# A planned attention kernel: order of the opening, four norms on ScalarE, new places

## The chip, the cores and the metric

One core of one Trainium2 chip. The metric is the device time of one execution in microseconds (us), lower is better.

## The reference

`x` is (4, 2048, 256) in FP32: 4 batches, 2048 tokens, width 256. Three residual steps:

```python
x = x + 0.5 * ffn(layernorm(x))      # 8 experts, top 2; an expert with more than cap tokens gives 0
x = x + attn(layernorm(x))           # 16 heads of 16, window of 128 each way, token 0 global
x = x + 0.5 * ffn(layernorm(x))
```

`cap` is int(1.25 * 8192 / 8) = 1280 tokens. An expert that gets more is left out as a whole (`keep = counts <= cap`). In attention, query and key may meet if they are at most 128 apart or one of them is token 0; logits are scaled by 1/4, softmax, times V, times Wo. `layernorm` has no gain or bias, eps 1e-5.

## The kernel before, in words

The kernel computes attention straight through and, beside it, the gate's logits for both expert steps; at the end a flag says whether any expert is kept. Only then are the experts computed and attention done over. In the profiled execution this part does not run: what is timed is attention, the logits, and the flag.

A batch is 16 tiles of 128 tokens in 4 chunks of 4 tiles; heads go in 4 groups of 4, so there are 16 groups (4 batches times 4), each over 16 tiles. The work of one chunk:

- EARLY: load x; MOMENTS per tile on VectorE (bn_stats, bn_aggr, L716, L718); RSTD on GpSimd (L730 to L743: rstd by pow, the shift); NORM per tile, (x - mean) * rstd into `xn`. In batch 0 all NORMs are on VectorE (L1387), in later batches tiles 0 and 1 on GpSimd (L1280), 2 and 3 on ScalarE (L1167).
- XT: two transposes of two tiles each on TensorE (L900) into one of two shared PSUM banks, emptied by ScalarE (XT_IN, L1191) into `xnT`.
- QK: q and k of a group of heads for one chunk, 4 parts of 8 matmuls (L965), into a shared bank. FP32 operands are then cut into three BF16 pieces: PIECE1 on ScalarE (L1209), REST on VectorE (L1463, which frees the bank), PIECE2 on ScalarE (L1224), PIECE3 on GpSimd (L1327).
- STACK: 12 DMAs stack the pieces along the contraction axis, as `q_stack` and `k_stack`. They are issued by SP. In group 0 five of the twelve are issued by ScalarE (L1218), in its own order between its other work.
- A: the logits of a strip of 128 queries of one head, 4 matmuls (L1076), in a ring of three PSUM banks; VectorE adds the mask and takes the row maximum (L1535, two records per strip). 1024 strips in all. The maxima are turned (TURN_MAX), split (MAX, PIECES) and laid into `q_stack` by 3 more DMAs (L870).
- B, 20 tiles behind A: the logits again, transposed and less the maximum (L1110), exp on ScalarE (L1259), masks CUT on GpSimd (L1339, L1344). PV, three tiles later (L1128), then TURN, OUT_ADD, OUT_RECIP, OUT_MULT.
- VALUES (L980) makes V; FIRST, in nine stages, is the row of token 0, which meets all keys.
- LATE: per chunk, once its batch's attention is done: TURN_ATTN (L933), PROJECT (L947), the residual on VectorE (PROJECT_IN, L1443), MOMENTS, RSTD, the second logits, STORE.

The order is written by `stages` and `schedule`. Time is counted in quarters: one quarter is one strip of A, 64 make a group, 256 a batch. The tables (`QK_AT`, `VALUES_AT`, `FIRST_AT`, `EARLY`, `LATE`, `LOAD_AT` and so on) give a quarter for each step; in batch 0 tables ending in `_OPENING` are used, and negative quarters lie ahead of the first strip. `schedule` sorts all steps into one list, and each engine runs through that list and takes its own steps in that order. An engine never goes past a step whose semaphore is not there. So the tables set only the order on each engine, and waiting sets the times. The two shared banks (`misc`) are handed out in list order too: a step gets the bank that was emptied longest ago, and waits (`claim`) until it is.

Ahead of the first real matmul TensorE runs `keep_busy(WARM)`: matmuls of ones by ones (L885, two records each) into a bank that nobody reads. `BUSY_XT[c][p]`, `BUSY_QK[c]` and `BUSY_A` put more of them before the transposes, the QKs of group 0 and the first strips; they are issued ahead of the waits of the step they stand before.

```python
def norm_engine(i, t):

    return "vector" if first and order[i][1] == 0 else NORM_ENGINES[t // 2]
```

ScalarE's order in the opening is: XT_IN of chunk 1 (twice), PIECE1, PIECE2, STACK 0 0, XT_IN of chunk 2 (twice), PIECE1, PIECE2 of it, XT_IN of chunk 3 (twice), STACK 0 1, PIECE1 of chunk 3, and so on. Chunks are counted from 1 in this text and from 0 in the code's tuples: A 2 2 is head 2 of tile 2.

## Time and profile before

| what | us |
|---|---|
| three timed runs | 842.47, 846.52, 848.89 |
| their median | 846.52 |
| the profiled execution, its own time | 843.41 |
| its span in the profile | 841.6 |

The span is from the first to the last instruction that the profiler recorded; the execution's own time has 1.8 us more around it. "Busy" is the union of an engine's instruction records; a busy TensorE is not TensorE at its peak, since the ends of matmuls are modelled. The chain of waits is followed back from the last instruction, at each step to what released it. The granted clock is 1.00 for 2.4 GHz and 0.50 for 1.2 GHz.

### The profile page before, as it was taken

How to read it: one execution, taken by the hardware profiler on the slowest of the kernel's cores; microseconds unless marked ns; L12 is line 12 of the kernel's file. 1: busy time of each engine (PE TensorE's matmuls, PEld its weight loads, DVE VectorE, ACT ScalarE, POOL GpSimd, SP SyncE). 2: the span in 40 equal slices, each digit the busy share in tenths (PEclk: the TensorE clock that was granted, in tenths of full speed). 3: DMA queues.
4: the chain of work that ended last, by engine and by line, in shares of the span. 5: the costliest groups of instructions: out<-in, count | busy, mean ns of one | idle time of the engine just before them, and what ended most of it. 6: DMA issues, size and time to landing. Idle time of an engine off the chain costs nothing.

```text
span 841.6 us, 50562 instructions
## 1 busy us (share of the span) xinstructions
PE 809.3 (96%) x21494; PEld 618.2 (73%) x21495; DVE 730.9 (87%) x2787; ACT 610.3 (73%) x1387; POOL 524.5 (62%) x888
## 2 busy tenths in 40 slices
PE   7899999999999999999999999999999999999997
PEld 7655767778788787677778777777778778776675
DVE  6899899998977899998987799998987789999864
ACT  3325778897877667888777766888787766788970
POOL 2355756896554556888554466789554465766772
PEclk9999999999999999999999999999999999999999
DMA  8342225332213235442222244533221323424003
GB/s 240 90 98 68 83 76 135 112 112 69 82 59 117 91 116 151 123 130 69 89 94 66 82 143 129 148 98 100 68 79 62 114 95 103 134 78 128 7 28 107
DMA packets 93210, 83.55 MB, mean 99 GB/s; under 512 B 17584, under 2 KB 92208, under 8 KB 92976
## 3 DMA queue, kind: packets, MB, share of 16 engines
q1 hardware_dynamic: 91376, 78.91, 30.7%
q8 instruction: 172, 2.82, 1.5%
q10 hardware_dynamic: 1600, 1.31, 0.8%
q14 instruction: 62, 0.51, 0.2%
HBM read 20.66 MB, written 8.39 MB: 35 GB/s over the span
## 4 chain that ended last, share of the span: by engine, by line
PE 76%; DVE 9%; ACT 6%; issue 3%; POOL 3%; SPq 1%; ACTq 1%; DMA 1%; DVEq 0%; POOLq 0%
PE bank L1128 15%; PE bank L1076 12%; PE bank L1110 12%; PE bank L965 11%; PE bank L947 7%; PE bank L980 6%; DVE bank L1535 5%; PE bank L1150 3%; ACT probs L1259 3%; PE bank L933 2%; PE bank L885 2%; PE bank L900 1%; ACT pieces L1209 1%; PE bank L1020 1%; DVE row_max L1535 1%
## 5 line engine op out<-in xcount | busy, mean ns | idle before, releaser
L1259 ACT ACTIVATE probs<-bank 128x384 f32<-128x384 f32 (+1 forms) x1024 | 457.1, 479 | 144.1 <-PE bank L1110 127.6
L1535 DVE CUSTOM_DVE_ANT_0 bank<-bank,con 128x288 f32<-128x288 f32 x1024 | 493.4, 514 | 58.4 <-PE bank L1076 52.4
L1076 PE MATMUL bank<-k_stack,q_stack 96*32 96x288 bf16 x4096 | 334.1, 288 | 7.1 <-DVE row_max L1535 4.2
L1110 PE MATMUL bank<-q_stack,k_stack 99*32 99x288 bf16 (+3 forms) x4096 | 326.3, 284 | 5.8 <-ACT probs L1259 2.1
L1128 PE MATMUL bank<-probs,v_sb 128*32 128x128 f32 x5888 | 314.5, 272 | 4.6 <-issue 1.7
L1339 POOL TENSOR_SCALAR_AFFINE_SELECT probs<-probs 128x512 f32<-128x512 f32 x240 | 154.7, 644 | 135.4 <-ACT probs L1259 134.4
L1128 PEld LDWEIGHTS bank<-probs,v_sb 128*32 128x32 f32 x5888 | 200.8, 110 | 34.3 <-issue 5.8
L1076 PEld LDWEIGHTS bank<-k_stack,q_stack 96*32 96x32 bf16 x4096 | 134.8, 95 | 68.1 <-DVE row_max L1535 25.2
L1110 PEld LDWEIGHTS bank<-q_stack,k_stack 99*32 99x32 bf16 x4096 | 131.1, 95 | 57.1 <-ACT probs L1259 34.4
L1344 POOL TENSOR_SCALAR_AFFINE_SELECT probs<-probs 128x512 f32<-128x512 f32 x240 | 152.8, 637 | 21.1 <-ACT probs L1259 21.1
L965 PE MATMUL bank<-xnT,wqk_sb 128*32 128x256 f32 x2048 | 160.3, 379 | 0.1
L1535 DVE DVE_READ_ACCUMULATOR2_ANT row_max<- 128x1 f32 x1024 | 143.6, 140 | 0.0
L1327 POOL TENSOR_TENSOR pieces<-rest,pieces 128x512 bf16<-128x512 f32 x64 | 74.6, 1166 | 62.1 <-ACT pieces L1224 62.1
L980 PE MATMUL bank<-wv_sb,xnT 128*32 128x272 f32 x1024 | 86.1, 393 | 0.6 <-DVE rest L1463 0.2
L947 PE MATMUL bank<-wo_sb,attnT 128*32 128x264 f32 x1024 | 73.9, 386 | 0.7 <-DVE x_ring L1443 0.4
L965 PEld LDWEIGHTS bank<-xnT,wqk_sb 128*32 128x32 f32 x2048 | 65.8, 110 | 5.2 <-ACT v_sb L1231 0.5
L1209 ACT ACTIVATE pieces<-bank 128x512 bf16<-128x512 f32 x64 | 38.4, 600 | 25.6 <-PE bank L965 24.4
L1463 DVE TENSOR_TENSOR rest<-bank,pieces 128x512 f32<-128x512 f32 x64 | 44.0, 688 | 8.2 <-ACT pieces L1209 8.0
L1224 ACT ACTIVATE pieces<-rest 128x512 bf16<-128x512 f32 x64 | 40.6, 634 | 8.6 <-DVE rest L1463 8.4
L1150 PE MATMUL bank<-con,o_raw 128*32 128x68 f32 x2048 | 44.5, 223 | 1.6 <-ACT o_raw L1266 1.6
L1266 ACT ACTIVATE o_raw<-bank 128x512 f32<-128x512 f32 x59 | 35.2, 596 | 11.8 <-PE bank L1128 11.7
L1356 POOL TENSOR_TENSOR glob_term<-v_all,p 128x272 f32<-128x272 f32 x64 | 41.6, 650 | 3.2 <-DVE v_all L1504 2.8
(124 smaller groups left out, 738.3 us busy)
## 6 DMA issues: line engine op xcount, KB each, us to landing
q_stack<-pieces SPq DMA_DIRECT2D x384, 64.0 KB
k_stack<-pieces SPq DMA_DIRECT2D x364, 64.0 KB
x_ring<-in_x SPq DMA_DIRECT2D x28, 512.0 KB, 5.3
out_x<-x_ring SPq DMA_DIRECT2D x15, 512.0 KB, 3.7
attn<-in_x SPq DMA_DIRECT2D x4, 512.0 KB, 6.2
wback_sb<-in_wback SPq DMA_DIRECT2D x8, 256.0 KB, 5.5
k_stack<-pieces ACTq DMA_DIRECT2D x20, 64.0 KB
q_stack<-neg_max SPq DMA_DIRECT2D x48, 16.0 KB, 2.4
```

Source lines behind the costliest of these rows:

```text
L947: last = pe.matmul(bank_of("PROJECT", i, t)[SP * s:SP * (s + 1), 0:D + E], attnT[:, t // 2, k, at:at + SP], wo_sb[:, k, :], start=(k == 0) ...
L965: last = pe.matmul(bank_of("QK", g, c)[SP * s:SP * (s + 1), 256 * half:256 * (half + 1)], wqk_sb[:, g % NG, k, SP * s:SP * (s + 1)], xnT[: ...
L980: last = pe.matmul(bank_of("VALUES", b, t)[SP * s:SP * (s + 1), 0:D + HD], xnT[:, k, at:at + SP], wv_sb[:, k, :], start=(k == 0), stop=(k ...
L1076: last = pe.matmul(a_ring[i % len(a_ring)][SP * s:SP * (s + 1), 0:WIN], q_stack[g % 2][0:KROWS, h, q:q + SP], k_stack[g % 2][0:KROWS, h, q ...
L1110: last = pe.matmul(score_bank(i)[SP * s:SP * (s + 1), start:final], k_stack[g % 2][0:SROWS, h, WINDOW + P * j + SP * s:WINDOW + P * j + SP ...
L1128: last = pe.matmul(o_bank[SP * h:SP * (h + 1), P * (i % 4):P * (i % 4 + 1)], v_sb[:, j, VW * head:VW * head + SP], probs[:, j % 4, h, P * ...
L1150: last = pe.matmul(bank_of("TURN", n)[SP * s:SP * (s + 1), HG * VW * i:HG * VW * (i + 1)], o_raw[:, at:at + SP], take, start=True, stop=True)
L1259: act.activation(probs[:, j % 4, h, c0:c1], score_bank(i)[:, c0:c1], ACT.Exp, scale=LOGIT_SCALE).then_inc(S["exp_ready"], 1)
L1327: pool.tensor_tensor(pieces[i % PIECES][:, 2, :], rest[:, :], pieces[i % PIECES][:, 1, :], ALU.subtract).then_inc(S["piece3_ready"], 1)
L1339: pool.affine_select(out=part, in_=part, compare_op=ALU.is_ge, fill=0.0, base=0, pattern=[[0, HG], [1, P]], channel_multiplier=-1).then_in ...
L1344: pool.affine_select(out=part, in_=part, compare_op=ALU.is_ge, fill=0.0, base=0, pattern=[[0, HG], [-1, P]], channel_multiplier=1).then_in ...
L1535: dve.tensor_tensor_reduce(out=a_ring[i % len(a_ring)][:, 0:WIN], in0=a_ring[i % len(a_ring)][:, 0:WIN], in1=mask, scale=1.0, scalar=con[: ...
```

## The change

It changes the tables that set the order, nearly all of them, and three rules. WARM goes from 31 to 27, the fillers before the second transpose of chunk 1 from 4 to 1, those before its QK from 3 to 1. `NORM_FIRST` puts tiles 2 and 3 of chunks 3 and 4 of batch 0 on ScalarE instead of VectorE (4 instructions). Batch 0 gets its own table `EARLY_FIRST` for MOMENTS, RSTD and NORM. The second copy of a transpose in batch 0 stands one quarter later. No other instruction is added, dropped or changed.

Worked out from the tables, the order of the opening on VectorE was, from the moments of chunk 2 on: REST of chunk 1, MOMENTS 2 0, NORM 1 0, NORM 1 1, MOMENTS 2 1, NORM 1 2, MOMENTS 2 2, MOMENTS 2 3, NORM 1 3, then MOMENTS of chunk 4 mixed with NORM of chunk 3, REST of chunk 2, NORM 2 3, NORM 3 0 to 3 3, seven strips, REST of chunk 3, strips to A 4 2, REST of chunk 4. It is now: MOMENTS 2 0, REST of chunk 1, MOMENTS 2 1, NORM 1 0, NORM 1 1, MOMENTS 2 2, MOMENTS 2 3, NORM 1 2, NORM 1 3, NORM 2 0, NORM 2 1, MOMENTS 3 0 to 3 3, REST of chunk 2, NORM 3 0, NORM 3 1, nine strips, REST of chunk 3, strips to A 4 3, REST of chunk 4. (First number: chunk from 0; second: tile.)

On ScalarE NORM 2 2 and 2 3 stand behind the copies of chunk 2 and ahead of its PIECE1; NORM 3 2 and 3 3 stand behind the copies of chunk 3 and ahead of the DMA issues of STACK 0 1 and of PIECE1 of chunk 3. PIECE2 of chunk 3 stands behind the first copy of chunk 4. On TensorE the QK parts of chunks 3 and 4 stand one to two strips later. On SP some loads and stores pass one stack or one MAX.

```diff
--- before.py
+++ after.py
@@ -349,9 +349,9 @@
         LEAD = 3
         STACK_DMAS = 2 * TERMS
         MAX_STACKED = 16 * 3
-        WARM = 31
-        BUSY_XT = ((0, 4), (0, 5), (0, 8), (0, 3))
-        BUSY_QK = (3, 4, 0, 0)
+        WARM = 27
+        BUSY_XT = ((0, 1), (0, 5), (0, 8), (0, 3))
+        BUSY_QK = (1, 4, 0, 0)
         BUSY_A = ((0, 0, 0, 1),)
 
 
@@ -372,35 +372,37 @@
 
             return (P if j == 0 else 0), (2 * P if j == NT - 1 else 3 * P)
 
-        QK_AT = (-43, -28, -10, 5, 23, 41, 53, 68, 83, 101, 118, 134, 149, 165, 178, 202)
+        QK_AT = (-43, -25, -10, 5, 23, 40, 53, 68, 83, 99, 118, 134, 149, 165, 179, 202)
         QK_APART = (2, 3, 2, 2, 2, 2, 1, 3, 1, 1, 1, 1, 1, 1, 2, 2)
         ONES_FROM = 2
         STACK_LAG = 20
-        VALUES_AT = (33, 48, 57, 61, 69, 80, 88, 94)
-        VALUES_APART = (2, 2, 1, 2, 2, 2, 1, 2)
-        VALUES_AT_OPENING = (36, 47, 57, 63, 66, 80, 89, 94)
-        VALUES_APART_OPENING = (1, 1, 1, 0, 2, 1, 1, 0)
+        VALUES_AT = (33, 47, 57, 61, 71, 80, 88, 94)
+        VALUES_APART = (2, 1, 0, 2, 2, 2, 1, 2)
+        VALUES_AT_OPENING = (36, 47, 57, 63, 67, 76, 89, 93)
+        VALUES_APART_OPENING = (1, 1, 1, 0, 2, 2, 0, 1)
         LOGITS_LAG = -2
-        FIRST_AT = (-16, -8, 15, 32, 50, 60, 96, 111, 135)
-        FIRST_AT_OPENING = (10, 22, 32, 44, 50, 60, 103, 106, 137)
-        FIRST_APART = (1, 2, 1, 4, 1, 3, 0, 1, 4)
-        EARLY_AT = (-79, -64, -49, -31)
-        EARLY = {'LOAD': -18, 'MOMENTS': (0, 3, 6, 7), 'RSTD': 10, 'NORM': (11, 13, 14, 18), 'XT': 19}
+        FIRST_AT = (-16, -9, 15, 32, 53, 60, 96, 111, 139)
+        FIRST_AT_OPENING = (10, 19, 32, 44, 50, 60, 103, 106, 138)
+        FIRST_APART = (1, 3, 1, 1, 0, 4, 0, 1, 0)
+        EARLY_AT = (-79, -64, -48, -31)
+        EARLY = {'LOAD': -20, 'MOMENTS': (-1, 3, 6, 7), 'RSTD': 9, 'NORM': (10, 13, 13, 18), 'XT': 19}
         NORM_ENGINES = ("gpsimd", "scalar")
-        EARLY_AT_OPENING = (-68, -49, -39, -30)
-        XT_AT_OPENING = (-55, -31, -18, 9)
-        QK_AT_OPENING = (-44, -26, 2, 14, 25, 39, 52, 69, 85, 98, 124, 131, 153, 162, 182, 201)
-        OPENING = {'ORDER_HEADS': -79, 'WBACK': -53, 'FOLD': 175, 'FILL': 21, 'QK_APART': 1, 'STACK': 5, 'STACKS': 12}
+        EARLY_FIRST = {'MOMENTS': (1, 3, 7, 7), 'RSTD': 7, 'NORM': (12, 13, 15, 15)}
+        NORM_FIRST = (('vector', 'vector'), ('vector', 'vector'), ('vector', 'scalar'), ('vector', 'scalar'))
+        EARLY_AT_OPENING = (-62, -47, -41, -29)
+        XT_AT_OPENING = (-50, -32, -16, 9)
+        QK_AT_OPENING = (-44, -25, 4, 15, 25, 39, 52, 70, 84, 98, 124, 131, 153, 165, 182, 201)
+        OPENING = {'ORDER_HEADS': -78, 'WBACK': -62, 'FOLD': 175, 'FILL': 13, 'QK_APART': 1, 'STACK': 7, 'STACKS': 11}
         LATE_AT = (95, 115, 131, 146)
         LATE_AT_END = (52, 68, 85, 102)
-        LATE = {'LOAD': -13, 'TURN_ATTN': 2, 'PROJECT': ((7, 8, 10, 10), (12, 12, 15, 15)), 'BASE': -13, 'MOMENTS': (12, 18, 18, 19), 'RSTD': 21, 'STORE': 25}
+        LATE = {'LOAD': -17, 'TURN_ATTN': 2, 'PROJECT': ((7, 8, 10, 11), (12, 12, 15, 15)), 'BASE': -15, 'MOMENTS': (12, 16, 19, 19), 'RSTD': 25, 'STORE': 27}
         LATE_END = {'TURN_ATTN': 0, 'PROJECT': ((6, 6, 8, 9), (12, 15, 15, 15)), 'BASE': -2, 'MOMENTS': (12, 16, 16, 23), 'RSTD': 35, 'STORE': 24}
-        LOAD_AT = (150, 164, 188, 214, 351, 346, 373, 388, 417, 427, 445, 459, 572, 610, 627, 635, 646, 678, 685, 717, 863, 869, 891, 907, 988, 1000, 1006, 1129)
-        STORE_AT = (381, 396, 400, 416, 618, 641, 659, 679, 878, 923, 916, 937)
-        WBACK_AT = (214, 471, 723)
+        LOAD_AT = (152, 155, 186, 215, 354, 350, 374, 380, 411, 414, 435, 450, 573, 608, 630, 632, 642, 673, 685, 718, 867, 876, 896, 906, 999, 995, 986, 1119)
+        STORE_AT = (371, 390, 396, 422, 628, 642, 654, 679, 882, 930, 919, 936)
+        WBACK_AT = (212, 469, 723)
         COUNT_AT = 16
         FLAG_AT = (6, 6)
-        OUT_AT = (-1, -1, 4, 3, -1, -1, -1, 1, -1, 8, 1, 0, 0, 1, 3, 0)
+        OUT_AT = (-1, -1, 4, 3, 0, -1, -1, 1, -1, 8, 1, 0, -1, 1, 3, 0)
         OUT = {'TURN': 0, 'ADD': 0, 'RECIP': 1, 'MULT': 2}
         MAX_AT = {'KEY0': -1, 'TURN_MAX': 1, 'MAX': 2, 'PIECES': 3, 'P0': -1, 'EXP0': 6}
 
@@ -429,13 +431,13 @@
                     early = BATCH * b + EARLY_AT[c] if b else EARLY_AT_OPENING[c]
                     late = BATCH * (b + 1) + (LATE_AT if b < nb - 1 else LATE_AT_END)[c]
                     moments = (LATE if b < nb - 1 else LATE_END)["MOMENTS"][0]
-                    order.append((early + EARLY["MOMENTS"][0], "EARLY", b, c, early))
+                    order.append((early + (EARLY if b else EARLY_FIRST)["MOMENTS"][0], "EARLY", b, c, early))
                     order.append((late + moments, "LATE", b, c, late))
             order = [item[1:] for item in sorted(order, key=lambda item: item[0])]
             ringed = [i for i, (phase, b, _, _) in enumerate(order) if phase == "LATE" or b]
 
             for i, (phase, b, c, at) in enumerate(order):
-                plan = EARLY if phase == "EARLY" else LATE if b < nb - 1 else LATE_END
+                plan = (EARLY if b else EARLY_FIRST) if phase == "EARLY" else LATE if b < nb - 1 else LATE_END
                 if first and i in ringed:
                     begun = LOAD_AT[ringed.index(i)]
                     end(begun, "LOAD", i)
@@ -462,11 +464,11 @@
                     end(at + plan["RSTD"], "RSTD", i)
                 if phase == "EARLY":
                     for t in range(4):
-                        opening(at + EARLY["NORM"][t], "NORM", i, t)
+                        opening(at + plan["NORM"][t], "NORM", i, t)
                     turn = at + EARLY["XT"] if b else XT_AT_OPENING[c]
                     for p in range(2):
                         begin(turn, "XT", i, p)
-                        opening(turn + 1, "XT_IN", i, p)
+                        opening(turn + 1 + (0 if b else p), "XT_IN", i, p)
             for n in range(NG * nb):
                 b, g = divmod(n, NG)
                 for c in range(4):
@@ -681,7 +683,7 @@
 
             def norm_engine(i, t):
 
-                return "vector" if first and order[i][1] == 0 else NORM_ENGINES[t // 2]
+                return NORM_FIRST[order[i][2]][t // 2] if first and order[i][1] == 0 else NORM_ENGINES[t // 2]
 
             def gates(i):
```

## Rows read from the trace of the kernel before

**Rows 1.** The page: busy time by engine, VectorE's strips (busy, mean ns, idle)
```profile
PE 809.3 (96%) x21494; PEld 618.2 (73%) x21495; DVE 730.9 (87%) x2787; ACT 610.3 (73%) x1387; POOL 524.5 (62%) x888
...
L1535 DVE CUSTOM_DVE_ANT_0 bank<-bank,con 128x288 f32<-128x288 f32 x1024 | 493.4, 514 | 58.4 <-PE bank L1076 52.4
```

**Rows 2.** Stretches: us, busy PE, PEld, DVE, ACT, POOL (records), clock, DMA share, GB/s
```profile
0.00:40.00 40.00, 33.84 (x430) 27.20 (x431) 28.10 (x103) 12.19 (x19) 13.35 (x29) 0.96 0.61 169
40.00:80.00 40.00, 37.74 (x787) 21.97 (x791) 39.14 (x158) 15.04 (x35) 18.86 (x21) 1.00 0.32 83
80.00:720.00 640.00, 627.97 (x17215) 488.28 (x17209) 568.25 (x2212) 499.93 (x1138) 419.07 (x713) 1.00 0.33 100
```

**Rows 3.** Chain that ended last, 0 to 41 us: start, length, what
```profile
1.15 9.55 PE bank L885 x62
...
13.13 1.91 PE bank L965 x32
...
18.42 0.35 DVE stats L716
...
20.29 0.39 DVE xn L1387
...
23.43 1.86 PE bank L965 x32
...
27.67 0.45 PE bank L900 x4
...
32.51 0.60 ACT pieces L1209
...
39.38 0.61 ACT pieces L1209
```

**Rows 4.** PE's fillers (us, PE, PEld busy, clock, DMA), and a transpose
```profile
7.00:10.60 3.60, 3.60 (x34) 3.50 (x32) 1.00 1.06 353
20.00:23.00 3.00, 1.93 (x10) 1.85 (x10) 0.50 0.90 101
...
18.48 0.66 PE L900 MATMUL bank<-con,xn 128*128 128x128 f32 x4 [3.48 <-DVE xn L1387]
```

**Rows 5.** VectorE in order of time, opening
```profile
8.53 1.38 DVE L1387 TENSOR_SCALAR xn<-attn,mean_var,rstd 128x256 f32<-128x256 f32 x4 [1.48 <-POOL rstd L733]
...
15.69 0.69 DVE L1463 TENSOR_TENSOR rest<-bank,pieces 128x512 f32<-128x512 f32 x1 [3.64 <-ACT pieces L1209]
...
29.50 0.52 DVE L1535 CUSTOM_DVE_ANT_0 bank<-bank,con 128x288 f32<-128x288 f32 x1
...
29.94 0.52 DVE L1535 CUSTOM_DVE_ANT_0 bank<-bank,con 128x288 f32<-128x288 f32 x1
...
33.13 0.69 DVE L1463 TENSOR_TENSOR rest<-bank,pieces 128x512 f32<-128x512 f32 x1 [0.82 <-ACT pieces L1209]
...
40.01 0.69 DVE L1463 TENSOR_TENSOR rest<-bank,pieces 128x512 f32<-128x512 f32 x1 [0.55 <-ACT pieces L1209]
```

**Rows 6.** Groups by line: normalising on VectorE (opening) and on ScalarE (later batches)
```profile
L1387 DVE TENSOR_SCALAR xn<-attn,mean_var,rstd 128x256 f32<-128x256 f32 x16 | 6.8, 468 | 2.7 <-POOL rstd L733 2.2 <-PE bank L900 0.6
...
L1167 ACT ACTIVATE xn<-x_ring,shift,rstd 128x256 f32<-128x256 f32 x24 | 14.3, 594 | 0.0
```

**Rows 7.** ScalarE and its DMA issues (ACTq), 26 to 41 us
```profile
28.15 0.60 ACT L1191 ACTIVATE xnT<-bank 128x512 f32<-128x512 f32 x1 [0.31 <-PE bank L900]
28.15 4.30 ACTq L1218 DMA_DIRECT2D k_stack<-pieces  x5
...
34.64 0.55 ACTq L1218 DMA_DIRECT2D k_stack<-pieces  x1
...
35.23 4.05 ACTq L1218 DMA_DIRECT2D k_stack<-pieces  x4
```

**Rows 8.** Waits of GpSimd and PE, 120 to 760 us: total, times, longest
```profile
POOL var_eps L730 <- DVE mean_var L718: 3.9, 9, 0.7
...
PE bank L1128 <- POOL probs L1339: 0.7, 1, 0.7
```

## The prediction

> **What bounds the kernel now.** I read the page first. TensorE (PE) is busy 96% of the 841.6 us span and VectorE (DVE) 87% [rows 1]. The middle of the kernel (80 to 720 us) has 640.0 - 628.0 = 12.0 us in which PE is idle; the first 40 us alone have 6.2 us, with every other engine far from full, and from 40 to 80 us DVE is busy 39.1 of 40 us [rows 2]. So three things set the end: a serial chain in the opening, DVE just behind it, and PE's plain work after that, which no order shortens. A time saved before DVE fills at about 40 us should move everything behind it, since what follows is issued in a fixed order against semaphores.
>
> So the chain of the opening is what I read closest [rows 3]. In it the reader is to see: 62 filler records of PE (31 matmuls) up to 10.70, then transposes with fillers between them, QK of the first chunk from 13.13, the pieces on ScalarE (ACT) and DVE, a DVE stretch of moments and normalisations up to 20.68, transposes and fillers up to 23.43, QK of chunk 2, fillers again, a last transpose up to 28.12, and from 28.15 on ACT: a copy, five DMA issues, PIECE1 at 32.51, REST on DVE at 33.13, then the same once more, to PIECE1 at 39.38 and REST at 40.01.
>
> **The opening, step by step.** (a) WARM drops by 4 matmuls, 8 records. The fillers at 7.0 to 10.6 run 34 in 3.60 us, 0.106 each [rows 4], so the first transpose comes 0.85 earlier, at 9.85. Its data is there: DVE normalises from 8.53, two tiles by about 9.3, four by 9.91 [rows 5]. The fillers before the second transpose go from 4 to 1, 6 records or 0.64 less, and it starts at about 10.5, behind the 9.91 at which its tiles are ready. QK needs the ACT copy of that transpose, 0.60 [rows 7], so it starts at about 11.6 where it started at 13.13. The fillers before QK (3 to 1) lie beside that copy and are worth nothing. Sum: 1.5 us earlier. It cannot be more, because the 9.91 and the copy are next in line.
>
> (b) MOMENTS of tile 0 of chunk 3 now stands ahead of REST. DVE is idle there (3.64 us before REST [rows 5]) and the chunk's load has most of the time since 5.8 to land, so it costs nothing and takes 0.55 from behind REST. But MOMENTS of tile 1 takes its place there, so the first transpose of chunk 2 gains nothing beyond 1.5. Behind it stood MOMENTS, NORM, MOMENTS, MOMENTS, NORM (18.42 to 20.68, 2.26 [rows 3]); now MOMENTS, MOMENTS, NORM, NORM, some 1.9, since the first MOMENTS is gone ahead and the rest stand side by side. The tiles of the second transpose are thus ready 1.9 earlier.
>
> (c) The stretch 20.0 to 23.0 ran at a granted clock of 0.50, that is 1.2 GHz: 10 fillers in 1.93 us, 0.193 against 0.106 [rows 4]. It came after PE had been idle from 15.04 to 18.48 [rows 3, 4]. The gap keeps its size, so I let the slow stretch come again at the same step, and carry 1.9 us to the end of the second transpose of chunk 3, 28.12 to 26.2. If the slow stretch missed the transpose and the fillers, both would take half (1.1 and 1.6 us there): 0.55 + 0.8 more, 3.3 in all. If it fell on QK instead, the gain would be 1.5. I keep 1.9, with 1.5 and 3.3 as ends.
>
> (d) Two tiles each of chunks 3 and 4 are normalised on ACT. DVE's 0.47 becomes ACT's 0.59 [rows 6]; ACT's row is of later batches, with x_ring as the source and the same 128x256 shape. For chunk 3 the two (1.2 us) lie in ACT's idle time before PIECE1 and cost nothing. For chunk 4 they stand between the copy of the last transpose and the five DMA issues. Those begin with the ACT instruction ahead of them (both at 28.15, [rows 7]) and take 4.30, and PIECE1 is queued behind them. The issues start at 26.25 + 0.5 + 0.55 = 27.3, end at 31.6, and PIECE1 comes at 31.65 instead of 32.51. So of 1.9 us some 1.1 is given back, and 0.86 is left. Ends: nothing given back (the norms lie under the issue time) and 1.2 given back.
>
> (e) REST of chunk 3 now stands two strips later in DVE's order. DVE idled 0.82 before it with 7 strips done; the strips cost 0.44 each (29.50 to 29.94) [rows 5]. Now 9 are done when REST runs. Against that PE's second transpose of chunk 4 still waits for the bank that REST frees, at about 32.9, so the tenth and eleventh strip can't run on freely: strip A 2 2 runs at about 33.75 instead of 35.05 (33.13 + 0.6 + 3 times 0.44), 1.3 earlier. For REST of chunk 4, ACT's copy (33.55) starts the next five issues, 4.64 from first to last [rows 7], so PIECE1 comes at 38.25 instead of 39.38, and DVE has one strip more done: 1.1 + 0.44 = 1.55 us earlier at 40 us. From there DVE is full and all shifts together. PIECE2 behind the first copy costs nothing, as REST is not done before the copy is.
>
> **The rest.** Behind the opening QK, VALUES, FIRST, PROJECT and MOMENTS move by a few places in each batch, some loads and stores pass one stack, and RSTD of the early chunks is one place earlier, a place being one strip, at most 0.8 us (841.6 over the 1024 strips of [rows 1]). No instruction is added or taken away. Where PE is full, an exchange on it is worth nothing; where it isn't, only the 12.0 us of [rows 2] can be won. The loads and stores that pass a stack wait for other data than it does; what SP loses or wins there the trace does not show, and the bounds cover it. I put all this at 0, with ends -4.0 (a third of the 12.0 won) and +3.2 (the second rival).
>
> Sum against the profiled execution: 843.41 - 1.55 = 841.9. That execution is 3.1 below the median 846.52, inside the spread 842.47 to 848.89; off the median the sum gives 845.0. I take the middle, 843.4.
>
> The Trainium skill has a rule that speaks about step (d): "DMA: Bandwidth & Descriptors", section "Issuing engines are not separate DMA queues", says that issuing on several engines only saves sequencer time, usually small beside the transfer. By it the ACT issues would hardly matter and 1.1 us would not be given back (840.8 from 843.41, 842.3 by the middle); the row with 4.30 us of issues ahead of PIECE1 says otherwise, and I go by the row.
>
> **Rivals.**
> 1. The clock takes the gain. With fewer fillers PE has less to do before each QK. For it: the clock did fall to 0.50 after the one long gap [rows 4]. Against: only 9 matmuls go, and the new gap before QK of chunk 1 is some 0.4 us. If the slow stretch covered QK of chunk 2 (1.86) as well as what it covers now, the QK would take up to 1.86 more, of which 1.55 eats the gain: time unchanged, 843.41 by the profile, 845.0 where the forecast has 843.4. The Trainium skill, "TensorE: Matmul & The Clock Gate", section "Part 1: The HAM clock gate (the "warmup" mystery)", has it that slow is the default and that activity releases it; by that rule taking fillers out is the wrong way. This rival has its chance from it and the row together.
> 2. The other side: GpSimd (POOL) blocked. RSTD of the early chunks of batches 2 to 4 waits for moments of DVE, whose last place is unchanged while RSTD's is one earlier. In 120 to 760 us it already waited 3.9 us in 9 of its 24 turns [rows 8]. Up to 0.8 more in each of 12 is 9.6 us of waiting on POOL, with the masks (CUT) of the probabilities queued behind it, and PE's PV behind them. PE's own wait for POOL there is 0.7 us [rows 8], so most of it is hidden. If a third comes through, 3.2: 843.41 - 1.55 + 3.2 = 845.1, 1.7 slower than before (846.6 where the forecast has 843.4). It decides from 1.55 us, a sixth of the added waiting, on.
> 3. The middle gains. If each of three batches recovers 1.0 to 1.3 us of its PE idle time (12.0 in 640 us) through the new places, the time is 3.0 to 4.0 lower: 838 to 839 by the profile, 840 to 841 where the forecast has 843.4. For it: nearly all tables of the batches are re-made. Against: PE is at 98% there.
> 4. The change doesn't do what it says: the norms on ACT give back all the opening saves. The ends of (c) and (d), 1.5 - 1.2, leave 0.3, and the strip ahead 0.4: 0.7 less, 842.7 by the profile, 844.3 where the forecast has 843.4, not told apart from my forecast by the time, only by the trace.
>
> **How the numbers follow.** Forecast with rival 4 0.50, rival 1 0.14, rival 2 0.14, rival 3 0.20, something larger of either sign 0.02. The range is 838.0 to 848.5: below, rival 3 with half of the runs' own spread; above, rival 2 with 2.2 of it. What a measurement can tell from no change is about 1%, 8.5 us; none of these cases reaches it alone, rival 3 on a low sample comes nearest. Hence faster 0.09, same 0.86, slower 0.05.
>
> **What would show it.** In the changed profile: the filler group 54 records; QK of chunk 1 at 11.6; the second transpose of chunk 2 by 19.9; 4 NORM records on ACT before 30 us, the latter two ending just before or beside the issues; PIECE1 of chunk 3 at 31.7, REST of chunk 4 at 38.9, PE idle in the first 40 us about 4.5 to 5. If REST of chunk 4 is not earlier than 39.5, the opening is wrong; if it is and the span isn't shorter by as much, it is the middle, and the waits of POOL for moments tell whether rival 2 is it.

## The result, and the profile after

The changed kernel takes **846.1 us** (median of 22 runs, 843.12 to 853.85), the kernel before 843.0 us (22 runs, 840.38 to 849.51). The ratio is **1.0033, 95% interval 1.0018 to 1.0049**: some 2.8 us slower by the means. I had forecast 1.6 us faster. The time lies inside my range; the sign is wrong.

The page's head and first block, after, as [rows 1]:

```profile
span 844.6 us, 50526 instructions
...
PE 810.7 (96%) x21476; PEld 613.5 (73%) x21477; DVE 731.4 (87%) x2783; ACT 614.0 (73%) x1391; POOL 524.8 (62%) x888
```

And the stretches, as [rows 2] (us, busy PE, PEld, DVE, ACT, POOL, clock, DMA share, GB/s):

```profile
0.00:40.00 40.00, 33.50 (x460) 26.79 (x462) 29.41 (x109) 14.99 (x24) 14.69 (x31) 0.91 0.65 174
40.00:80.00 40.00, 38.87 (x807) 22.34 (x808) 38.87 (x157) 17.58 (x41) 19.42 (x22) 1.00 0.32 86
80.00:720.00 640.00, 626.70 (x17141) 481.92 (x17133) 567.58 (x2203) 498.23 (x1130) 415.65 (x706) 1.00 0.33 99
720.00:830.00 110.00, 103.11 (x2946) 77.31 (x2948) 89.92 (x302) 82.60 (x198) 75.04 (x131) 0.98 0.22 71
```

Busy time says little here. PE is busy 626.7 of the middle's 640 us where it was 628.0; four NORMs have gone from DVE to ACT and nothing else shows. What shows is the place of the work in time. The chain of waits in the opening, as [rows 3]:

```profile
9.39 0.63 PE bank L902 x4
10.02 0.22 PE bank L887 x2
10.24 0.44 PE bank L902 x4
10.90 1.91 PE bank L967 x32
...
16.25 1.12 PE bank L902 x4
17.36 2.13 PE bank L887 x10
19.50 0.85 PE bank L902 x4
20.35 1.71 PE bank L887 x8
22.06 1.86 PE bank L967 x32
...
26.30 0.44 PE bank L902 x4
```

QK of chunk 1 starts at 10.90 where it started at 13.13. REST on DVE, as [rows 5]:

```profile
13.46 0.69 DVE L1465 TENSOR_TENSOR rest<-bank,pieces 128x512 f32<-128x512 f32 x1 [0.81 <-ACT pieces L1211]
...
31.33 0.69 DVE L1465 TENSOR_TENSOR rest<-bank,pieces 128x512 f32<-128x512 f32 x1
...
37.79 0.69 DVE L1465 TENSOR_TENSOR rest<-bank,pieces 128x512 f32<-128x512 f32 x1
```

REST of chunk 4 comes at 37.79 instead of 40.01, with one strip more done. So at 40 us the changed kernel is 2.7 us ahead, more than forecast, and at the end it is 3.0 us behind. To see where that went I took the start of the same strip on DVE (L1535 before, L1537 after, 1024 records each in the timeline) in each profile and subtracted that of before:

| strip | 0 | 64 | 256 | 448 | 512 | 640 | 768 | 896 | 1003 | 1023 | end |
|---|---|---|---|---|---|---|---|---|---|---|---|
| changed kernel | -1.9 | -3.0 | -3.0 | -0.8 | -1.9 | -2.6 | -0.9 | +0.1 | 0.0 | +2.3 | +3.0 |

The opening's 3 us hold through batch 1 and are lost in batches 2 to 4 and in the tail. The tail's part is one stop of TensorE, here in its timeline (start, length, what, idle before and what ended it):

```profile
773.97 0.30 PE L1112 MATMUL bank<-q_stack,k_stack 99*32 99x288 bf16 x4
774.09 0.29 PE L1078 MATMUL bank<-k_stack,q_stack 96*32 96x288 bf16 x3
776.30 0.40 PE L1078 MATMUL bank<-k_stack,q_stack 96*32 96x288 bf16 x1 [1.91 <-issue]
776.30 0.82 PE L1130 MATMUL bank<-probs,v_sb 128*32 128x128 f32 x8
```

PE stands still for 1.91 us after three of the four matmuls of one strip. The fourth needs no tile that the third did not, and the profile shows no semaphore that it waited for ("issue"). Then the clock falls, in PE's windows:

```profile
776.30:779.70 3.40, 3.40 (x61) 0.51 0.03 8
779.70:782.00 2.30, 2.30 (x76) 0.99 0.00 0
```

3.4 us at 0.51 (1.2 GHz) do the work of 1.7 us at full clock. Stop and slow stretch together are 3.6 us, a little more than the span's whole loss.

### The profile page after: what moved, and what is told of

It reads as the page before. It is cut to its first block, busy times and chain, and to the rows that moved or that the text cites. A ratio compares the mean times of both kernels' runs of the same rounds, so it can differ in the third digit from the quotient of the medians.

```text
span 844.6 us, 50526 instructions
## 1 busy us (share of the span) xinstructions
PE 810.7 (96%) x21476; PEld 613.5 (73%) x21477; DVE 731.4 (87%) x2783; ACT 614.0 (73%) x1391; POOL 524.8 (62%) x888
## 4 chain that ended last, share of the span: by engine, by line
PE 71%; DVE 14%; ACT 5%; issue 4%; POOL 3%; SPq 1%; DMA 1%; ACTq 0%; POOLq 0%; DVEq 0%
PE bank L1130 15%; PE bank L1112 12%; PE bank L1078 12%; PE bank L967 11%; DVE bank L1537 8%; PE bank L949 6%; PE bank L982 6%; PE bank L1152 3%; ACT probs L1261 3%; PE bank L935 2%; DVE row_max L1537 2%; PE bank L902 1%; DVE rest L1465 1%; DVE stats L718 1%; ACT pieces L1211 1%
## 5 line engine op out<-in xcount | busy, mean ns | idle before, releaser
L1537 DVE CUSTOM_DVE_ANT_0 bank<-bank,con 128x288 f32<-128x288 f32 x1024 | 495.0, 516 | 65.2 <-PE bank L1078 58.7
L1537 DVE DVE_READ_ACCUMULATOR2_ANT row_max<- 128x1 f32 x1024 | 144.8, 141 | 0.0
L982 PE MATMUL bank<-wv_sb,xnT 128*32 128x272 f32 x1024 | 83.2, 393 | 0.5 <-DVE rest L1465 0.2
L949 PE MATMUL bank<-wo_sb,attnT 128*32 128x264 f32 x1024 | 76.0, 387 | 0.7 <-DVE x_ring L1445 0.4
L1152 PEld LDWEIGHTS bank<-con,o_raw 128*32 128x32 f32 x2048 | 36.0, 108 | 10.1 <-ACT o_raw L1268 7.6
```

Of the source, the lines that this page charges most:

```text
L949: last = pe.matmul(bank_of("PROJECT", i, t)[SP * s:SP * (s + 1), 0:D + E], attnT[:, t // 2, k, at:at + SP], wo_sb[:, k, :], start=(k == 0) ...
L982: last = pe.matmul(bank_of("VALUES", b, t)[SP * s:SP * (s + 1), 0:D + HD], xnT[:, k, at:at + SP], wv_sb[:, k, :], start=(k == 0), stop=(k ...
L1152: last = pe.matmul(bank_of("TURN", n)[SP * s:SP * (s + 1), HG * VW * i:HG * VW * (i + 1)], o_raw[:, at:at + SP], take, start=True, stop=True)
L1537: dve.tensor_tensor_reduce(out=a_ring[i % len(a_ring)][:, 0:WIN], in0=a_ring[i % len(a_ring)][:, 0:WIN], in1=mask, scale=1.0, scalar=con[: ...
```

## The experiments

18 kernels ran, in five comparisons, each with its own runs of the kernel before (medians 844.18, 843.58, 842.86, 844.31 and 842.59). "Mean" is the mean of the kernel's runs less that of before in the same comparison. Single executions of one kernel scatter by about 2 us (standard deviation), so a mean of this table has a standard error of 0.5 to 0.9 us, and two kernels in different comparisons are told apart from some 2 us on.

| kernel | median us | ratio, 95% interval | mean |
|---|---|---|---|
| open_only | 841.9 | 0.9965 [0.9943, 0.9986] | -2.5 |
| batch_only | 850.4 | 1.0064 [1.0040, 1.0087] | +5.6 |
| after_loads_late | 848.72 | 1.0051 [1.0026, 1.0076] | +4.5 |
| before_loads_late | 846.63 | 1.0029 [1.0004, 1.0055] | +2.3 |
| open_sp_new | 845.77 | 1.0015 [0.9991, 1.0038] | +1.2 |
| open_pe_new | 845.76 | 1.0019 [0.9999, 1.0040] | +2.0 |
| open_el_new | 842.29 | 0.9986 [0.9968, 1.0004] | -1.7 |
| after_sp_back | 844.4 | 1.0007 [0.9988, 1.0026] | +0.4 |
| open_qk_new | 843.29 | 0.9988 [0.9966, 1.0010] | -0.6 |
| open_values_new | 844.11 | 1.0002 [0.9971, 1.0032] | +0.8 |
| open_values_first_new | 844.3 | 1.0014 [0.9985, 1.0042] | +0.8 |
| open_out_new | 844.18 | 1.0001 [0.9974, 1.0027] | +0.2 |
| open_again | 842.19 | 0.9985 [0.9961, 1.0009] | -1.7 |
| open_warm_back | 843.03 | 0.9991 [0.9968, 1.0015] | -0.9 |
| open_norm_dve | 842.55 | 0.9982 [0.9961, 1.0002] | -1.3 |
| open_loads_spread | 843.28 | 0.9977 [0.9957, 0.9997] | -1.3 |
| after_qk_back | 845.74 | 1.0036 [1.0014, 1.0058] | +3.0 |
| after_sp_qk_back | 843.25 | 1.0024 [1.0005, 1.0042] | +1.1 |

**Opening or batches.** `open_only` is the changed kernel with the twelve tables of batches 2 to 4 (QK_AT, VALUES_AT, VALUES_APART, FIRST_AT, FIRST_APART, OUT_AT, EARLY_AT, EARLY, LATE, LOAD_AT, STORE_AT, WBACK_AT) of before; `batch_only` is the kernel before with those twelve of the changed kernel.

> The changed opening with the batch tables of before. The two profiles compared strip by strip say: the opening saves about 2.0 us up to the first strip, 2.7 up to the REST of chunk 4 and some 3.0 by the end of batch 1. Theory A (the batch tables lose it, about 1.1 us in batch 2 and some more later, and the tail has a stall of its own): this kernel is 2 to 3 us faster than before. Theory B (what loses is a stall of 1.9 us of TensorE at 774.4 us, in the middle of a strip's four matmuls, while three loads of 512 KB are in flight: TensorE has run out of instructions and its next block of them stands behind the loads; where the blocks end depends on how many filler matmuls the opening has): the stall, with up to 3.4 us at half clock behind it, is here too, and the time is within 1 us of before or above it.

> The opening of before (31 fillers, all normalisations on VectorE) with the changed batch tables. Theory A (batch tables): slower than before by 4 to 6 us, most of it between strips 336 and 450 of each batch. Theory B (instruction block behind the loads, set by the opening's instruction count): the blocks end where they did before, no stall above 1 us in 770 to 780 us, and the time is 0 to 1.5 us above before.

Measured: the opening alone wins 2.5 us, and 1.7 when built and timed anew; the batches' tables alone lose 5.6. (`batch_only`'s -0.6 at strip 64 grows to +3.7 at strip 448 and +9.9 at strip 1003.) So the loss is in the batches' tables, as theory A had it (4 to 6 us), and the opening's gain comes through where they are left alone.

**The last loads.** A first idea was that the three loads before the tail's stop cause it and that they could simply stand later:

```diff
-LOAD_AT = (..., 999, 995, 986, 1119)
+LOAD_AT = (..., 1034, 1033, 1032, 1119)
```

and in `before_loads_late` 988, 1000, 1006 became 1032, 1033, 1034.

> The changed kernel, with the loads of the last batch's chunks 1 to 3 (3 times 512 KB) issued after the 3 DMAs of MAX 15 (about 789 us) instead of right after STACK 15 3 (769 us). Nothing needs them before 808 us. Theory B: the stall of 1.9 us at 774.4 us and the half clock behind it go, the kernel is 2.5 to 4 us faster than the changed one, so about 0.5 us faster than before. Theory A: within 1 us of the changed one, 2 to 3 us slower than before.

> The kernel before with the same three loads moved behind MAX 15. There the chain shows 3.4 us for the last stack DMA and TensorE waiting 1.1 us for it at 771.2 us, with the same loads in flight. Theory B: the loads' burst costs this kernel only that: 0.5 to 1.5 us faster than before. Rival: the burst costs nothing but moves, same as before within 0.5 us.

Both got slower, which neither theory had. The stop did not go, it moved with the loads and grew. PE in the timeline of `after_loads_late`:

```profile
795.61 0.65 PE L1130 MATMUL bank<-probs,v_sb 128*32 128x128 f32 x8 [3.08 <-issue]
```

and in that of `before_loads_late` (the kernel before has no such stop in its tail; its wait of 1.09 at 771 us is one for keys and queries, and stays here with 1.18):

```profile
793.18 0.30 PE L1110 MATMUL bank<-q_stack,k_stack 99*32 99x288 bf16 x2 [2.94 <-issue]
```

That points at the loads. The page of the changed kernel has a DMA queue of kind "instruction" (packets, MB, share), and 172 of its packets of 16 KB fit PE's 21476 + 21477 records at 256 instructions each (167.8):

```profile
q8 instruction: 172, 2.82, 1.6%
```

Between 45 us and the end six in ten start 3.5 to 4.9 us apart, the mean is 4.7, and one in ten is over 6.0. The DMA view of the changed kernel, cut to 767.0 to 773.7, shows the three loads and no such packet:

```profile
GB/s 6 0 220 141 12 6 12 6 12 6 0 141 239 12 0 226 159 6 24 55 0 0 31 147 208 220 373 373 379 373 391 373 391 379 385 385 391 391 385 385
...
q1 hardware_dynamic: 1259, 1.21, 53.8%
issues: line engine op xcount, KB each, median us to landing
x_ring<-in_x SPq DMA_DIRECT2D x3, 512.0 KB, 4.9
```

The same view from 773.7 to 775.0 has it, among 368 GB/s of other traffic:

```profile
q8 instruction: 1, 0.02, 5.3%
```

I listed the stops of PE of over 0.7 us behind 45 us in all profiles, with the last instruction packet ahead of their end. The longest of eight kernels:

| kernel | stop at | us | since the packet before | packet's start to the stop's end |
|---|---|---|---|---|
| changed kernel | 774.4 | 1.91 | 7.3 | 2.5 |
| open_only | 771.4 | 1.12 | 7.1 | 2.2 |
| open_sp_new | 509.5 | 1.68 | 7.1 | 2.6 |
| open_pe_new | 134.1 | 1.44 | 7.2 | 2.6 |
| open_el_new | 563.3 | 1.08 | 8.2 | 2.6 |
| batch_only | 494.6 | 2.80 | 9.3 | 2.7 |
| before_loads_late | 790.2 | 2.94 | 8.0 | 2.4 |
| after_loads_late | 792.5 | 3.08 | 8.5 | 2.4 |

All of over 1.1 us that are put down to "issue" end 2.2 to 3.1 us after a packet, and that packet came 5.1 to 9.3 us behind the one before it. That alone proves little, as a packet in five comes over 5.5 us behind the one before it and few of them stop PE. The records can be counted, though, and that settles it. Take the number of PE's records (matmuls, weight loads and the sequencer's own) before a stop, less 256 for each instruction packet that started ahead of the last one before the stop's end. In the twenty profiles there are 160 stops of over 0.15 us put down to "issue" between 45 and 800 us, and this number is 449, 450 or 451 for every one of them: they all stand at the edge of a block of 256 instructions, in whatever strip that edge falls. PE's 750 idle times put down to a semaphore lie anywhere from 189 to 583 by the same count, 22 of them at 449 to 451. 157 of the 160 end 2.2 to 3.5 us after a packet's start. So these stops, the small ones too, are PE out of instructions; that is shown.

The same count, taken where a packet starts, tells how late it is by PE's own progress: the median is 252 records, which leaves PE some 200 (my estimate from 43,543 records in 844.6 us: 3.8 us of work). At the packet ahead of the changed kernel's stop of 1.91 us it is 430, the highest of its profile; at the packets of the stops of 2.80, 2.94 and 3.08 us it is 449, so PE was dry before they started. All 16 stops of over 1.1 us follow a packet at 365 or more. With under 50 GB/s of other traffic in the 3 us ahead of a packet the mean is 244, with over 330 GB/s it is 335. Moving the loads moved the stop, and packets start later under traffic; both are shown. That a packet waits in the DMA engines behind a load is the likely way, but no view shows its waiting. Ahead of 15 of the 16 a transfer of 512 KB was in flight; at the other (`batch_only`, 338.0, 1.21 us) two loads and a store had been issued from 327.4 us on and keys and queries followed. Ahead of its stop at 494.6 `batch_only` has SP issue two loads back to back, where the kernel before has keys and queries between them:

```profile
485.42 3.82 SPq L838 DMA_DIRECT2D x_ring<-in_x  x2
```

**Which tables.** On top of `open_only` the changed tables were put in by kind: those of SP's transfers (`open_sp_new`: LOAD_AT, STORE_AT, WBACK_AT), of TensorE (`open_pe_new`: QK_AT, VALUES_AT, VALUES_APART, FIRST_AT, FIRST_APART, OUT_AT), of statistics, norms and projections (`open_el_new`: EARLY, EARLY_AT, LATE). `after_sp_back` is the changed kernel with SP's three of before.

> The changed opening with the batches' places of before, except the places of SyncE's transfers (LOAD_AT, STORE_AT, WBACK_AT), which are the changed kernel's. With the places of before throughout, this kernel took 0.9965 of before. Theory S (the changed order of SyncE's 512 KB transfers starves TensorE of instructions): it gives back most of the 6.8 thousandths between that and the changed kernel, so about 1.000 to 1.003, with stops of TensorE of over 1 us in the middle of a strip. Theories E (VectorE's and GpSimd's places of statistics and norms) and P (TensorE's places): 0.995 to 0.998, no such stop.

> The changed opening, the batches' places of before except TensorE's (QK_AT, VALUES_AT, VALUES_APART, FIRST_AT, FIRST_APART, OUT_AT), which are the changed kernel's. Theory P: about 1.000 to 1.003 of before. Theories S and E: 0.995 to 0.998.

> The changed opening, the batches' places of before except those of the statistics, norms and projections (EARLY, EARLY_AT, LATE), which are the changed kernel's. Theory E: about 1.000 to 1.003 of before, with the turning of a group's maxima waiting some 1 us for VectorE's row of maxima behind a statistic in several groups, or GpSimd's cut behind a RSTD. Theories S and P: 0.995 to 0.998 and no such waits beyond those of before.

> The changed kernel with LOAD_AT, STORE_AT and WBACK_AT of before. Theory S: it falls to about 0.997 of before (the changed kernel took 1.0033), and the stop of 1.91 us at 774 us and the half clock after it are gone. Theories E and P: 1.001 to 1.004.

Against `open_only` and `open_again` the transfers cost 3 to 4 us, TensorE's places 4, each to about 1 us, the statistics and norms nothing. `after_sp_back` gives 2.4 back, less than theory S had said: 1.0007, not 0.997. Its stop at 774 us is down to 0.76. So S and P are both right in part, E is out.

PE's idle time at the edges of instruction blocks (45 to 800 us, stops over 0.15 us, one profile each) is 2.7 us in the kernel before, 2.8 and 2.9 in `open_only` and `open_again`, 5.6 in `open_sp_new`, 5.7 in `open_pe_new`, 4.9 in the changed kernel and 9.7 in `batch_only`. So TensorE's places seem to work in part through late instructions too. It does not come out everywhere: `after_sp_back` has 5.8, and the kernels with only one kind of TensorE's places 2.0 to 4.1. Over the twenty kernels this idle time goes with the mean time (correlation 0.7), and PE's waits for other engines and DMAs do not (-0.2).

TensorE's places were then split, again on top of `open_only`:

> The changed opening, the batches' places of before except QK_AT, which is the changed kernel's. The kernel with all of TensorE's new places lost about 4.5 us to the one with none in its strips of batches two to four, always at the same strips (about +0.6 at strips 240 to 300 and -0.8 at 304, +1 at 432, -0.8 at 480, +1.2 at 544, +1 at 752, +0.6 at 800). If the queries' and keys' places cause it, this kernel shows those steps and takes about 1.001 of before; if not, none of them and 0.996 to 0.998.

> The changed opening, the batches' places of before except VALUES_AT and VALUES_APART, which are the changed kernel's. If the values' places cause the loss of TensorE's new places: about 1.001 of before and steps at the same strips of each batch; if not, 0.996 to 0.998.

> The changed opening, the batches' places of before except VALUES_AT, VALUES_APART, FIRST_AT and FIRST_APART, which are the changed kernel's. Against the kernel with the values' places alone it tells what the first products' places do: if they cause the loss of TensorE's new places, about 1.001 of before where the values' places alone give 0.997; if neither, both 0.996 to 0.998.

> The changed opening, the batches' places of before except OUT_AT, which is the changed kernel's: the turn of the result of groups 4 and 12 stands one quarter away. If that causes the loss of TensorE's new places, about 1.001 of before; I expect none of it, 0.996 to 0.998.

The four times alone decide little (0.9988 to 1.0014, each +-0.003). The strips do show a mechanism for QK_AT. At the end of two groups DVE takes the row of maxima with the global key (KEY0). In `open_qk_new`, DVE's timeline:

```profile
345.73 1.16 DVE L1524 TENSOR_TENSOR row_max<-row_max,s0T 128x64 f32<-128x64 f32 x1
346.78 0.51 DVE L1537 CUSTOM_DVE_ANT_0 bank<-bank,con 128x288 f32<-128x288 f32 x1
```

and GpSimd's beside it:

```profile
345.62 1.16 POOL L1329 TENSOR_TENSOR pieces<-rest,pieces 128x512 bf16<-128x512 f32 x1
346.76 1.22 POOL L1282 TENSOR_SCALAR xn<-x_ring,mean_var,rstd 128x256 f32<-128x256 f32 x1
```

An instruction of 64 elements a partition takes 1.16 us and ends with GpSimd's subtraction. In the changed kernel it is 0.84, and PE, next in line, waits for it:

```profile
347.85 0.30 PE L1088 MATMUL bank<-con,row_max 128*32 128x128 f32 x2 [1.04 <-DVE row_max L1524]
```

The line's own view gives the least, median and longest of its 16 records in ns; the longest is 547 in the kernel before, 842 in the changed one, 1219 in `open_qk_new`, and in `after_qk_back` 273:

```profile
L1524 DVE TENSOR_TENSOR row_max<-row_max,s0T x16: 246/264/273, 60.9 to 780.4; 128x64 f32<-128x64 f32 x16
```

So the wait is real and QK_AT makes it. But is it the loss? The last two kernels put QK_AT back in the changed kernel, alone and with SP's three tables:

> The changed kernel (1.0033 of before) with QK_AT of before. If the queries' and keys' places put VectorE's row of maxima (0.84 us at 347 and 546 us, where GpSimd's subtraction of 1.16 us runs beside it) and TensorE's wait of 1.04 us behind it, the row takes 0.55 us at most, the wait is under 0.3 us, and the time is 1 to 2 us less: 1.001 to 1.002. If the wait has another cause it stays.

> The changed kernel with LOAD_AT, STORE_AT, WBACK_AT and QK_AT of before. If the two named mechanisms are most of the loss: 0.998 to 0.999, as the changed opening with the batches' places of before (0.9965 and 0.9985 in two measurements) and no stop of TensorE over 1 us but the one near 773 us. If the loss is spread over all of TensorE's places: 1.000 to 1.001, as with the transfers alone put back (1.0007).

The wait of 1.04 us is gone, the time is not less: 1.0036. With the transfers put back too it is 1.0024, not 0.998. The strips say why: in `open_qk_new` strips 544 to 559 take 1.0 us more than before and strips 560 to 575 take 0.7 less. The wait is mostly caught up at once.

To use all comparisons together I fitted the means of the fourteen kernels that differ by whole tables (least squares, weighted by their errors) by a sum of six parts:

| part | us | standard error |
|---|---|---|
| opening | -1.5 | 0.3 |
| SP's transfers | +2.5 | 0.5 |
| QK_AT | +0.3 | 0.4 |
| values and first products | +1.9 | 0.5 |
| turns of the result (OUT_AT) | +1.1 | 0.6 |
| statistics, norms, projections | -0.7 | 0.4 |

`open_values_new`, which has only half of the fourth part, counts for the whole of it. No kernel is more than 1.0 us off this sum; for the changed kernel it gives +3.5, measured +2.8.

**The opening's parts.** `open_again` is `open_only` unchanged; `open_warm_back` has WARM, BUSY_XT and BUSY_QK of before; `open_norm_dve` has all of NORM_FIRST on "vector"; `open_loads_spread` spreads the last burst:

```diff
-LOAD_AT = (..., 988, 1000, 1006, 1129)
+LOAD_AT = (..., 964, 980, 1006, 1129)
```

> The same kernel as open_only (the changed opening, the batches' places of before), built and timed anew. If the opening's gain carries to the end, 0.994 to 0.999 of before again; if the first measurement was luck, 1.000 to 1.002. Its profile shows how much the same program varies between two executions: less than 1 us strip for strip, apart from the opening's slow clock, if the steps that I read from single profiles are real.

> open_only with WARM, BUSY_XT and BUSY_QK of before (31 waiting products ahead of the first transposition in place of 27, more between the parts). The prediction put their removal at 1.5 us at the first queries and keys. If it holds, the first queries and keys start 1.5 us later than in open_only (10.9 us) and the strips 0.5 to 1.5 us later to the end, 0.998 of before; if the opening waits for the loads or for VectorE rather than for these products, no difference in the strips.

> open_only with the last two tiles of chunks three and four normalised on VectorE as before, at their new places. The prediction held that the tiles on ScalarE give back 1.1 us in the opening (PIECE1 of chunk three behind them) and give VectorE one more strip per norm moved. If that holds, the first strip comes 0.5 to 1.0 us earlier here; if, as the profile of the changed kernel suggests, ScalarE has room beside its five transfers, the strips come 0 to 1 us later than in open_only: four norms of 0.47 us on VectorE, about 1 us of them on the path.

> open_only with the last three loads apart (LOAD 28 ahead of the third and LOAD 29 ahead of the fourth set of key and query transfers of the last group, LOAD 30 behind them as before), in place of three back to back. Theory S' (an instruction block of TensorE that falls into a burst of 512 KB loads comes late, and TensorE stops in the middle of a strip): the stop of 0.8 to 1.9 us near 771 us, which every kernel with the changed opening shows at the same strip, goes, no two blocks near it lie over 6 us apart, and the time is 1 us less, about 0.995 to 0.997 of before. Rival (the stop is a wait of the strip for something else): it stays. Third: the loads hold up the last keys and queries and the last strips come later than in open_only.

`open_again` shows what one profile is worth: its strips differ from those of `open_only` by 0.3 at strip 64 and by 2.3 at strip 544. A step of under about 1 us in a single pair of profiles proves nothing; steps that return at the same strip in all kernels with a table do.

`open_warm_back`'s chain has QK of chunk 1 just where before has it:

```profile
12.02 0.44 PE bank L902 x4
12.45 0.67 PE bank L887 x6
13.12 1.91 PE bank L967 x32
```

and `open_again`'s, with the new filler counts:

```profile
1.14 8.39 PE bank L887 x54
9.53 0.52 PE bank L902 x4
10.05 0.22 PE bank L887 x2
10.27 0.44 PE bank L902 x4
10.71 0.22 PE bank L887 x2
10.93 1.91 PE bank L967 x32
```

The fillers are 2.2 us there, and 0.8 us in the means (-0.9 against -1.7 in the same comparison, not told apart by the time alone). Taking the norms back to DVE changes the time by nothing measurable; QK of chunk 3 starts 0.7 us later (27.8, 27.1 in `open_again`).

`open_loads_spread` does away with the stop at 771 us, and PE now stops where the first of the loads has gone:

```profile
757.01 0.31 PE L1130 MATMUL bank<-probs,v_sb 128*32 128x128 f32 x3 [1.23 <-issue]
```

The packet ahead of it came 6.9 us behind the last, where I had expected none over 6. Its mean is that of `open_norm_dve` in the same comparison, -1.3: nothing won. The stop went where a load met an instruction packet again.

## Why the prediction was wrong

**The step that failed is "The rest. ... I put all this at 0".** I argued that no instruction is added and that where PE is full an exchange on it is worth nothing. The whole of it is +5.6 us measured alone and +4.3 behind the opening (2.8 + 1.5 of the fit), above even my end of +3.2. Two things were missing from my argument. First, I looked at the transfers only for SP's own waiting ("what SP loses or wins there the trace does not show, and the bounds cover it") and not at whom a 512 KB load stands in front of. With the new places of the transfers PE's instructions come late: +2.5 us by the fit. Second, an exchange on a full engine can cost although it can't gain: a stop of PE is lost for good unless slack follows it, and 12.0 us of idle in 640 us leaves little. Of that part (+3.3 in the fit) KEY0 beside GpSimd's subtraction was seen, and the test says that it is not where the time goes; `open_pe_new` has 2.8 us more idle at block edges than `open_only`, in one profile. Which of the places of values, first products and turns does it, and how, is **open**.

**The opening's total was right, by luck: its terms were not.** Forecast -1.55, by the fit -1.5 +-0.3, by `open_only` and `open_again` -2.5 and -1.7. That 846.1 lies in my range is luck too. The range spans 10.5 us, and I took 845.0 for the kernel before, from three runs and a profile, where 22 runs give 843.0.

- (a) Fillers: forecast 1.5, measured 2.2. I said that the fillers before QK lie beside ACT's copy and are worth nothing. In both chains QK starts when those fillers end, 0.67 us behind the transpose before and 0.22 now: PE did not wait for that copy (10.05 to 11.31 for both copies, QK from 10.90). In the code the first half of QK waits only for the first copy. So these fillers were worth 0.45; most of the rest is the warm group, whose eight records moved its end by some 1.2 (10.70 before, 9.53 in `open_again`) and not by 0.85.
- (b) The second transpose of chunk 2 was forecast by 19.9 and comes at 19.50; right, although the first one starts at 16.25, 2.2 earlier and not 1.5.
- (c) The slow stretch came again, but not at the same step. It begins at about 15.2 and lasts twice as long as the 3.4 us of before:

```profile
15.20:22.00 6.80, 5.75 (x28) 0.50 0.63 122
```

The first transpose of chunk 2 takes 1.12 instead of 0.66 and its fillers 2.13. The end of the second transpose of chunk 3 is at 26.74, forecast 26.2. In the profiles of `open_again`, `open_loads_spread` and `open_norm_dve` QK of chunk 2 is at 20.8 to 21.1 instead of 22.06, with a clock of 0.83 instead of 0.76 over 10 to 20 us. So rival 1, the clock takes the gain, was right in kind: it took about 1 us in some executions, and the extra 0.7 of (a) outweighed it.
- (d) ACT's norms: 1.1 us "given back" was wrong, the true size is 0. ACT's timeline after, as [rows 7]:

```profile
26.77 0.60 ACT L1193 ACTIVATE xnT<-bank 128x512 f32<-128x512 f32 x1 [0.31 <-PE bank L902]
26.89 0.55 ACTq L1220 DMA_DIRECT2D k_stack<-pieces  x1
27.26 0.59 ACT L1169 ACTIVATE xn<-attn,shift,rstd 128x256 f32<-128x256 f32 x1
27.48 0.62 ACTq L1220 DMA_DIRECT2D k_stack<-pieces  x1
27.75 0.59 ACT L1169 ACTIVATE xn<-attn,shift,rstd 128x256 f32<-128x256 f32 x1
28.14 1.91 ACTq L1220 DMA_DIRECT2D k_stack<-pieces  x3
30.70 0.60 ACT L1211 ACTIVATE pieces<-bank 128x512 bf16<-128x512 f32 x1 [2.36 <-PE bank L967]
```

The norms run between and beside the issues, and PIECE1 waits 2.36 us for PE, not for ACT. This was my own lower end. The size of a norm (0.59 on ACT) was right. Here the Trainium skill's rule that I set aside, that issuing takes little beside the transfer ("DMA: Bandwidth & Descriptors", "Issuing engines are not separate DMA queues"), gave the better answer for the path, although the five issues do fill 3.2 us of ACT's queue: nobody waited for them.
- (e) REST of chunk 4: forecast 38.9, measured 37.79, with the strip ahead as forecast.

**The other rivals.** Rival 2 was the one on the right side, with 0.14, and it is refuted. GpSimd's wait for moments fell from 3.9 us in 9 [rows 8] to 1.6 in 4:

```profile
POOL var_eps L732 <- DVE mean_var L720: 1.6, 4, 0.5
```

and putting RSTD's new place into `open_only` (`open_el_new`) costs nothing. Its forecast, 846.6, is close to the measured 846.1 for another reason. Rival 3, the middle gains, went the other way. Rival 4 fell with (d).

**What had spoken for it in the rows of before.** The page of before has the same instruction queue, and its timeline a stop of 1.00 us put down to "issue" at 442.95, at the edge of a block too. I read neither, since such a stop names no engine.

## What to carry to other kernels

Where PE is 98% busy, re-placing work without adding any is not worth nothing: in this case it lost 4.3 us, since each new meeting of a big load with PE's instruction fetch can stop it. Price a moved 512 KB transfer by what else uses the DMA engines then, instruction packets included, not only by its own queue. And measure an opening and a middle apart: here the opening of the change with the middle of before beats both kernels (0.9965 and 0.9985 of before in two comparisons; the second alone is not clear of 1).

## What the runs showed of the hardware that I had not expected

**PE can run dry.** PE's instructions come in 16 KB packets some 4.7 us apart; with transfers of 512 KB in flight a packet starts up to 9.3 us behind the last one, and PE stops for up to 3.1 us, in the middle of a group. It stops only at the edge of a block, after every 256 instructions (160 of 160 stops). So work added or taken away far ahead moves the stop: 12 of the 16 profiles with the new filler counts have one of 0.76 us or more at strip 1010, those four with the old counts (before, `before_loads_late`, `batch_only`, `open_warm_back`), whose edges lie 36 records elsewhere, have none there. To find it in a trace, look for idle time put down to "issue" inside a group of matmuls, at a multiple of 256 records from the last such stop. The Trainium skill ("Runtime: NRT & Kernel Launch", "Instruction fetch mechanics") says that code is refilled in blocks of 16 KiB on a DMA queue of its own and that crossing a block is mostly hidden. The block and the queue agree with the 172 packets of the profile; hidden it is not beside these loads.

**The clock after a stop.** At the end of the stop of 1.91 us PE's granted clock fell to 0.50 for 3.4 us, near the end of that of 3.08 us for 6.8 us. Behind those of 2.94 and 2.80 us a stretch of 3.4 us at 0.50 began 0.3 and 0.7 us later, and so behind one of 1.59 (`open_qk_new`); behind one of only 1.08 us (`open_el_new`) the clock fell before the stop had ended. Behind stops of 1.12, 1.59 and 1.86 us it stayed 1.00 (`open_only`, `open_norm_dve`, `open_out_new`). In three profiles (`open_pe_new`, `after_sp_back`, `open_values_new`) it fell for 3.4 us at 789.0 to 791.9 with no stop of over 0.7 us in the 6 us ahead; PE had been busy 4.7 to 5.0 us of the 6.0 to 6.3 us ahead, as it had in the kernel before (5.05 of 6.0), where the clock stayed at 1.00. A slow stretch of 3.4 us costs up to 1.7 us, so it is probably one source of the 2 us scatter.

**Two memories in one instruction.** KEY0, with both inputs in SBUF, took 0.25 to 0.28 us with GpSimd idle, 0.81 to 1.22 beside GpSimd's subtraction (11 times in the twenty profiles), and 0.25 to 0.55 beside GpSimd's normalising of 1.22 to 1.29 us begun 0.03 to 0.5 us earlier. The Trainium skill ("SBUF — State Buffer", "Who interferes with whom") has it that a VectorE instruction with two SBUF inputs contends with a GpSimd instruction that reads SBUF, and it calls their shared ports an exclusive lock. Beside the subtraction the two end within 0.12 us of each other, which agrees; beside the normalising KEY0 was over at least 0.45 us before GpSimd was, so there it was not held for the whole instruction.
